# Gate and up of a ternary feed-forward with the weights stationary: the hidden layer comes out with its units on the partitions

## The chip, the cores and the metric

The kernel runs on one core of a Trainium2 chip. The metric is device time in microseconds (us) of one execution, taken as the median of several. Lower is better.

## The reference

16 sequences of 100 tokens (T = 1600 tokens, 512 features) pass a cross-attention and then a feed-forward layer; the change is in the feed-forward alone.

```python
x = x + _L0_xattn_ref(_layernorm(x), ctx_1024, ...)       # 16 heads of 128, 361 keys
x = x + _L0_ffn_ref(_layernorm(x), w_gate, w_up, w_down)  # 512 -> 2048 -> 512

def act_quant(x):      # per token, 8 bits
    scale = 127.0 / jnp.clip(jnp.max(jnp.abs(x), axis=-1, keepdims=True), EPS)
    return jnp.clip(jnp.round(x * scale), -128.0, 127.0) / scale
def weight_quant(w):   # one scale for the matrix, values -1, 0, 1
    scale = jnp.clip(jnp.mean(jnp.abs(w)), EPS)
    return jnp.clip(jnp.round(w / scale), -1.0, 1.0) * scale
def h_bitlinear(x, w): # fwht: Walsh-Hadamard transform over the whole last axis
    return jnp.einsum('bsh,oh->bso', act_quant(fwht(x)), weight_quant(w))
gate, up = h_bitlinear(h, w_gate), h_bitlinear(h, w_up)
return h_bitlinear(jax.nn.silu(gate) * up, w_down)
```

So after gate and up the hidden layer (2048 units for each token) is itself Hadamard-transformed, scaled by the largest value of each token, rounded to 8-bit integers, and multiplied by the ternary down weights.

## The kernel before, in words

Three stages follow each other: the queries, the attention, and `feed_forward` (L1254), which begins near 1027 us of the span. Only `feed_forward` is changed, apart from four semaphores that nobody waits for and that become one.

The feed-forward works on 12 tiles of 128 tokens and one last tile of 64 (t = 0 to 12). It is a software pipeline written out by hand. `step(i)` (one for each engine: L1463 POOL, L1618 PE, L1746 ACT, L1963 DVE) holds work of up to four tiles at once: gate and up, the hidden transform and the second rounding of tile i+1, down of tile i, residual, norm and first rounding of tile i+2, and the output projection of tile i+3. Every engine works its list in order; semaphores alone order the engines among each other.

TensorE's list in a step: `gate_up(i+1, 0..3)`, 30 matmuls of `out_proj(i+2)`, two `hidden_T`, `down(i)`, then `rotate_hidden(i+1, 0)`, `hidden_T(2)`, `rotate_hidden(1)`, `hidden_T(3)`, `norm_T(i+2)`, `rotate_hidden(2)` and `(3)`, `rotate_in(i+2)`, 12 matmuls of `out_proj(i+3)`, `q1_T(i+2)` and 6 more of `out_proj(i+3)`.

`gate_up(t, j)` (L1527) holds the turned integers q1T (128 features x 128 tokens, bf16) stationary and moves 512 columns of ternary weights (fp8) past them, 4 feature chunks for gate and 4 for up. So tokens lie on the partitions of PSUM, and the scale of a token is one number per partition. ACT takes silu of the gate bank with that scale (`silus`, L1743), and DVE multiplies the up bank by its scale and by that (`hidden`, L1898), into `hid`.

The Hadamard transform of the 2048 units is cut in two. Its upper part (which halves are added and subtracted) is done as butterflies on DVE and POOL: `rotate_within` (L1907), `rotate_pair1` (L1914) and `rotate_across` (L1920) on DVE, `rotate_pair0` (L1447, L1450) and its own `rotate_across` (L1456) on POOL. `hid` and `half_rot` are both in the SBUF tile `stage`, by which the profile names them. The lower part (256 wide) is done on PE by `rotate_hidden` (L1598) against a constant matrix, and for that the units must lie on partitions: `hidden_T` (L1588) transposes each 512 columns into the PSUM tiles psT, ACT rounds them to a high part (`high_hT`, L1689), and DVE takes the rest, psT minus the high part (`low_hT`, L1801). DVE then takes each token's peak (`peak`, L1859), `scales2` makes the scale, ACT and DVE round (`round2`, `ints2`), and a DMA turns the integers for `down`.

DVE's list behind the butterflies: residual and statistics of tile i+2, `low_hT(0)`, `norm`, `rotate_halves` (xr, L1832), `low_hT(1)`, `peak(0)`, `low_hT(2)`, `peak(1)`, `low_hT(3)`, `low_xT`, `peak(2)`, `peak(3)`, `scales1(i+2)`, `scales2(i+1)`, `ints1`, `ints2`. POOL's list: `rotate_pair0`, `rotate_across`, the inverse deviation (L1423), `low_o(i+3)` (L1428, the low part of the attention's output, 2048 values on each partition, released by `rotate_halves`), `result` (L1461) and two copies.

The last tile has 64 tokens: `gate_up_halves` (L1557) puts two halves of the units side by side in the array, `hidden_T_halves` (L1566) turns them.

Of the kernel before, what the change touches and what calls it, by code (L numbers as in the profile page):

```python
# [53 lines left out]
def build(nc, x, ctxT, ctx_k, wq, wk, wv, wo, gq, gk, w_ff, ident_in, had_in, out):  # L54
# [4 lines left out]
    with ExitStack() as top:  # L59
# [10 lines left out]
        passed = {e: sem(e + "_passed") for e in ("sp", "act", "dve", "pe")}  # L70
# [1183 lines left out]
def feed_forward(nc, sbt, sem, passed, bank0, ident, neg_half, w127, o_in, d_stored, d_first, x, x_in, xT0, wo_hi, wo_lo, had_in, o_dram,  # L1254
# [10 lines left out]
    with ExitStack() as ctx:  # L1265
# [13 lines left out]
        al, ald = sb("al", [P, 2]), sb("ald", [P, 1])  # L1279
# [21 lines left out]
        p_out, p_xT, p_rx, p_q1T, p_gu, p_hT, p_rh, p_down = (  # L1301
            s(f"p3_{n}") for n in ("out", "xT", "rx", "q1T", "gu", "hT", "rh", "down"))
# [5 lines left out]
        a_q1T, a_sil, v_h, g_pair0, v_pair1, v_r2, g_r2 = (s(n) for n in ("a3_q1T", "a3_sil", "v3_h", "g3_pair0", "v3_pair1",  # L1308
                                                                                  "v3_r2", "g3_r2"))
        v_cross, a_half = s("v3_cross"), s("a3_half")  # L1310
# [106 lines left out]
        def _(pool):  # L1417
# [61 lines left out]
        def _(pe):  # L1479
# [37 lines left out]
            def q1_T(t):  # L1517
# [3 lines left out]
                if due(t * NB):  # L1521
                    pe.wait_ge(v_hT, t * NB)
                for c in range(DC):
                    last = nc.tensor.transpose(psTb[1][:, c * P:(c + 1) * P], q1[:, c * P:(c + 1) * P], ident_b[:])
                last.then_inc(p_q1T, 1)

            def gate_up(t, j):  # L1527
# [18 lines left out]
            def gate_up_halves(t, j):  # L1546

                if j == 0:
                    pe.wait_ge(a_q1T, t + 1)
                pe.wait_ge(a_mag[1], 2 * t - 1 + j)  # L1550
                pe.wait_ge(v_h, t * NB + j - 1)
                apart(pe, pe_passed)
                for k in range(2):
                    for c in range(DC):
                        for g in range(2):
                            col = (j + g * NB // 2) * DIM
                            last = nc.tensor.matmul(psB[g * TH:(g + 1) * TH, 2 * j + k, :], q1T[:, c, g * TH:(g + 1) * TH],  # L1557
                                                    wt[:, k, c, col:col + DIM], start=(c == 0), stop=(c == DC - 1),
                                                    tile_position=(0, g * TH))
                last.then_inc(p_gu, 1)  # L1560

            def hidden_T_halves(t, n):
                pe.wait_ge(v_pair1, t * 6 + 5 + n)
                pe.wait_ge(a_q1T, t + 1)
                for c in range(DC):
                    last = nc.tensor.transpose(psT[n][:, c * P:(c + 1) * P], hid[:, n, c * P:(c + 1) * P], ident[:])  # L1566
                last.then_inc(p_hT, 1)
# [11 lines left out]

            def hidden_T(t, n):  # L1580
                if n % 2 == 0:
                    pe.wait_ge(g_r2 if n else v_r2, t + 1)
                if n < 2:
                    pe.wait_ge(a_q1T, t + 1)
                else:
                    pe.wait_ge(v_hT, t * NB + n - 1)
                for c in range(DC):
                    last = nc.tensor.transpose(psT[n % 2][:, c * P:(c + 1) * P], half_rot[:, n, c * P:(c + 1) * P], ident[:])  # L1588
                last.then_inc(p_hT, 1)
# [28 lines left out]
            def step(i):  # L1618
                if isinstance(i, int) and i == -2:
# [3 lines left out]
                    q1_T(0)  # L1623
                    out_proj(1, range(9, FIRST))
                    return
                if i == TILES - 2:
                    for j in range(NB // 2):
                        gate_up_halves(i + 1, j)
                    busy(psA, 7)
                    down(i, 0, TILES)  # L1630
                    hidden_T_halves(i + 1, 0)
                    hidden_T_halves(i + 1, 1)
# [36 lines left out]
                if real(i + 2):  # L1669
                    q1_T(i + 2)  # L1670
                if real(i + 3):
# [6 lines left out]
        def _(act):  # L1678
# [13 lines left out]
            def copy_half(t, n):  # L1692
                act.wait_ge(p_hT, t * NB + n + 1)
                nc.scalar.activation(hid[:, 2 + n, 0:DIM // 2].rearrange("p (c t) -> p c t", t=TH),  # L1694
                                     psT[n][:].rearrange("p (c g t) -> p c g t", g=2, t=TH)[:, :, 1, :], ACT.Copy
                                     ).then_inc(a_half, 1)

            def high_halves(t, n):
                act.wait_ge(v_cross, 2 * n + 2)
                if n == 0:  # L1700
                    act.wait_ge(p_rh, t * NB)
                nc.scalar.activation(hT_hi[:, n * DC:(n + 1) * DC, :].rearrange("p c t -> p (c t)"), half_rot[:, 2 + n, :],  # L1702
                                     ACT.Copy).then_inc(a_hT, 1)
# [7 lines left out]
            def round1(t):  # L1711
                act.wait_ge(v_scale[0], 5 * t + 4)
# [11 lines left out]

            def copy_q1T(t):
                act.wait_ge(p_q1T, t + 1)
                if due(t * NB):
                    act.wait_ge(p_gu, t * NB)
# [8 lines left out]
            def silus(t, blocks):  # L1737
                act.wait_ge(v_scale[0], 5 * t + 5)
                for j in blocks:
                    act.wait_ge(p_gu, t * NB + j + 1)  # L1740
                    if due(t * NB + j - 1):
                        act.wait_ge(v_h, t * NB + j - 1)
                    nc.scalar.activation(sil[:, j % 2, :], psB[:, 2 * (j % 2), :], ACT.Silu, scale=al[:, 0:1]  # L1743
                                         ).then_inc(a_sil, 1)

            def step(i):  # L1746
                if i == TILES - 2:
                    silus(i + 1, range(NB // 2))
                    for n in range(NB // 2):
                        copy_half(i + 1, n)  # L1750
                    for n in range(NB // 2):
                        high_halves(i + 1, n)
# [3 lines left out]
                for j in range(NB):  # L1756
                    if real(i + 1):
                        silus(i + 1, (j,))
# [5 lines left out]
                if real(i) and not last_tile(i):  # L1764
                    scale_down(i)
                if real(i + 1):
                    high_hT(i + 1, 2)
                    high_hT(i + 1, 3)
                if real(i + 2) and i > -2:
# [18 lines left out]
        def _(dve):  # L1788
# [50 lines left out]
            def scales(i, t, peaks, n, factor, weight):  # L1839

                c = slice(i, i + 1)
                norm_n = float(n) ** -0.5
                if due(t * (i + 1)):
                    dve.wait_ge(a_mag[i], t * (i + 1))
                nc.vector.tensor_reduce(mx[:, c], peaks, axis=AX.X, op=ALU.max, apply_absolute_value=True).then_inc(v_scale[i], 1)
                dve.wait_ge(v_scale[i], 5 * t + 1)
                nc.vector.tensor_scalar(am[:, c], mx[:, c], norm_n, EPS, ALU.mult, ALU.max).then_inc(v_scale[i], 1)
                dve.wait_ge(v_scale[i], 5 * t + 2)
                nc.vector.reciprocal(rc[:, c], am[:, c]).then_inc(v_scale[i], 1)
                dve.wait_ge(v_scale[i], 5 * t + 3)  # L1850
                nc.vector.tensor_scalar(sq[:, c], rc[:, c], 127.0 * norm_n, None, ALU.mult).then_inc(v_scale[i], 1)
                nc.vector.tensor_scalar(factor, weight, am[:, c], None, ALU.mult).then_inc(v_scale[i], 1)
# [204 lines left out]
```

## Time and profile before

| | |
|---|---|
| median of 3 runs | 1418.27 us (1416.5 to 1418.69) |
| span of the profiled execution | 1415.7 us |
| its granted TensorE clock | mean 0.994 |
| PE busy | 1384.3 us, 98% of the span |
| DVE busy | 933.8 us, 66% |
| ACT busy | 940.2 us, 66% |
| POOL busy | 517.2 us, 37% |
| the feed-forward | from 1027 us to the end |

The profile gives no time of its own for the profiled execution besides its span from the first to the last instruction; the median of the runs is 2.6 us above that span. A busy share says how long an engine had an instruction under way. Matmuls overlap in it: their ends are modelled, so what one costs is the distance between two starts. In a row of the timeline the first number is the start, the second the time to the end of the last instruction of the row, "x8" the number of instructions merged, and the bracket the idle time before it with the instruction that ended it. In a row of windows the numbers are the busy time of each engine with its count of instructions, then the granted TensorE clock (1.00 is full speed), the DMA share and GB/s.

### The profile page before, as it was taken

The numbers are of one execution on the slowest core, as the hardware profiler recorded it, in microseconds if no ns is written. First come the engines' busy times: TensorE is split into PE (matmuls) and PEld (weight loads), VectorE is DVE, ScalarE is ACT, GpSimd is POOL, SyncE is SP. The second block draws the span as 40 slices with busy tenths as digits, with TensorE's granted clock in tenths as the row PEclk, the third lists the DMA queues.
The fourth block names the chain that finished last, engine by engine and source line by source line (L and its number), as shares of the span: only waits on it lengthen the run. The fifth ranks groups of instructions, "written<-read, shape, count | busy, mean of one in ns | idle before, by whom it ended". The sixth has DMA issues, their size and how long they took to land. (4 is left out here: it accounts for less than half of the span.)

```text
span 1415.7 us, 25806 instructions
## 1 busy us (share of the span) xinstructions
PE 1384.3 (98%) x8407; PEld 1192.2 (84%) x8407; DVE 933.8 (66%) x2399; ACT 940.2 (66%) x2072; POOL 517.2 (37%) x323
## 2 busy tenths in 40 slices
PE   8999988999999999999999999999989999999998
PEld 8889867999999999999999999998867677776775
DVE  5222036667777777777777777766457677776775
ACT  4566558888888888888888888887533433343332
POOL 0033324432233223332323332324645465655551
PEclk9999999999999999999999999999989999999999
DMA  6867823334443443444344344325443322233211
GB/s 219 215 189 220 226 54 91 100 111 117 128 112 114 134 128 114 116 124 134 107 124 117 113 133 128 106 82 172 126 153 79 86 60 67 61 97 75 60 30 42
DMA packets 173492, 165.05 MB, mean 117 GB/s; under 512 B 81440, under 2 KB 149040, under 8 KB 171568
## 3 DMA queue, kind: packets, MB, share of 16 engines
q1 hardware_dynamic: 166448, 150.82, 38.5%
q10 hardware_dynamic: 6912, 12.59, 2.7%
q8 instruction: 69, 1.13, 0.3%
q14 instruction: 63, 0.52, 0.1%
HBM read 123.44 MB, written 33.01 MB: 111 GB/s over the span
## 5 line engine op out<-in xcount | busy, mean ns | idle before, releaser
L764 POOL TENSOR_TENSOR rk_sp<-ms_sp,neg_half 76x10 f32<-76x10 f32 (+1 forms) x128 | 238.5, 1880 | 567.0 <-DMA ms_sp<-ms 567.0
L1194 DVE CUSTOM_DVE_ANT_0 sc<-psS,rk 100x361 f32<-100x361 f32 x256 | 136.4, 533 | 97.1 <-PE psS L839 71.3
L986 ACT ACTIVATE pr<-ex,ri 100x361 f32<-100x361 f32 x256 | 153.6, 600 | 63.6 <-DVE ri L1184 63.6
L979 ACT ACTIVATE ex<-sc,nb,rq_all 100x361 f32<-100x361 f32 x256 | 175.9, 687 | 7.8 <-DVE nb L1203 7.8
L867 PE MATMUL psZ<-pT_hi,cK_hi 120*128 120x400 f32 (+1 forms) x384 | 133.3, 347 | 0.0
L867 PE MATMUL psZ<-pT_hi,cK_lo 120*128 120x400 f32 (+1 forms) x384 | 132.4, 345 | 0.0
L867 PE MATMUL psZ<-pT_lo,cK_hi 120*128 120x400 f32 (+1 forms) x384 | 132.2, 344 | 0.0
L852 PEld LDWEIGHTS psP<-ident,pr 100*120 100x120 f32 (+1 forms) x768 | 80.2, 165 | 43.5 <-issue 35.3
L839 PE MATMUL psS<-ring_hi,q_hi 128*100 128x362 f32 x256 | 97.0, 379 | 5.0 <-DVE mx L1194 5.0
L852 PE MATMUL psP<-ident,pr 100*120 100x100 f32 (+1 forms) x768 | 96.5, 261 | 4.0 <-ACT pr L986 4.0
L1176 DVE TENSOR_TENSOR pT_lo<-psP,pT_hi 121x600 fp32r<-121x600 f32 x128 | 99.0, 773 | 1.5 <-ACT pT_hi L1010 1.5
L882 PE MATMUL psNV<-z,wv_sb 128*128 128x200 f32 x504 | 97.2, 336 | 0.8 <-issue 0.8
L1184 DVE RECIPROCAL ri<-rs 100x1 f32<-100x1 f32 x256 | 41.3, 161 | 85.5 <-ACT ex L979 81.5
L1689 ACT ACTIVATE hT_hi<-psT 128x512 fp32r<-128x512 f32 x48 | 27.5, 596 | 99.8 <-PE psT L1588 99.8
L961 ACT ACTIVATE ring_hi<-bank 128x362 fp32r<-128x362 f32 x128 | 60.6, 473 | 44.1 <-PE bank L815 42.6
L1542 PE MATMUL psB<-wt,q1T 128*128 128x512 fp8e4 x384 | 86.6, 379 | 0.0
L815 PE MATMUL bank<-cT_hi,wk_hi 128*128 128x362 f32 x256 | 85.3, 333 | 1.0 <-DVE ring_lo L1129 1.0
L815 PE MATMUL psK<-cT_hi,wk_hi 128*128 128x362 f32 x256 | 85.0, 332 | 0.7 <-DVE ring_lo L1129 0.7
L1010 ACT ACTIVATE pT_hi<-psP 121x600 fp32r<-121x600 f32 x128 | 84.7, 662 | 0.0
L882 PEld LDWEIGHTS psNV<-z,wv_sb 128*128 128x128 f32 x504 | 83.0, 190 | 1.2 <-issue 1.1
L839 PE MATMUL psS<-ring_hi,q_lo 128*100 128x362 f32 x256 | 84.0, 328 | 0.0
L839 PE MATMUL psS<-ring_lo,q_hi 128*100 128x362 f32 x256 | 83.9, 328 | 0.0
(295 smaller groups left out, 3947.6 us busy)
## 6 DMA issues: line engine op xcount, KB each, us to landing
rk<-rk_dram SPq DMA_DIRECT2D x64, 564.1 KB
q_dram<-q_out SPq DMA_DIRECT2D x64, 200.0 KB, 4.3
q_in<-q_dram SPq DMA_DIRECT2D x64, 200.0 KB, 5.2
o_dram<-o SPq DMA_DIRECT2D x64, 200.0 KB, 5.4
stage<-in_w_ff SPq DMA_DIRECT2D x12, 1024.0 KB, 6.3
w_in<-in_w_ff ACTq DMA_DIRECT2D x48, 256.0 KB, 2.4
o_in<-o_dram SPq DMA_DIRECT2D x12, 1024.0 KB, 5.9
cT_in<-in_ctxT SPq DMA_DIRECT2D x15, 361.0 KB, 5.4
```

What stands on the lines that cost most here:

```text
L764: nc.gpsimd.tensor_tensor(rk_sp[:, cols], ms_sp[:, cols], neg_half[0:HG * SKR, :].to_broadcast([HG * SKR, n]), op=ALU.pow).then_inc(g_rk, 1)
L815: last = nc.tensor.matmul(psK[h % 2][:, 0:SKP], w[:, c, col:col + D], x[:, slot, c, :], start=(n == 0), stop=(n == 3 * CC - 1))
L839: last = nc.tensor.matmul(psS[0:SQ, 0:SKP], w[:, u % 2, cols], x[:, u % NG, h, :], start=(i == 0), stop=(i == 2))
L852: last = nc.tensor.transpose(psP[0:KW[i], k, i * SQ:(i + 1) * SQ], pr[:, 2 * half + k, KO[i]:KO[i] + KW[i]], ident[0:SQ, 0:SQ])
L867: last = nc.tensor.matmul(psZ[c][:, 0:UQ], w[0:KW[i], b % 2, i, c * P:(c + 1) * P], x[0:KW[i], u % 2, i, :], start=(n == 0), stop=(n == 8))
L882: last = nc.tensor.matmul(bank[:, k * 2 * SQ:(k + 1) * 2 * SQ], wv_sb[:, c, col:col + D], z[:, first % 4:first % 4 + 2, c, h * SQ:(h + 1) ...
L979: nc.scalar.activation(ex[:, h % 2, :], sc[:, h % 2, :], ACT.Exp, bias=nb[:, h % 2:h % 2 + 1], scale=factor(n), accum_out=rs[:, h % 2:h % ...
L986: nc.scalar.activation(pr[:, h, :], ex[:, h % 2, :], ACT.Copy, scale=ri[:, h % 2:h % 2 + 1]).then_inc(a_pr, 1)
L1010: nc.scalar.activation(two_heads(pT_hi, u, half), psP[0:KW[0], :, 0:3 * SQ].rearrange("p k (i q) -> p k i q", q=SQ), ACT.Copy).then_inc(a_ ...
L1176: nc.vector.tensor_tensor(two_heads(pT_lo, u, half), psP[0:KW[0], :, 0:3 * SQ].rearrange("p k (i q) -> p k i q", q=SQ), two_heads(pT_hi, u ...
L1194: nc.vector.tensor_tensor_reduce(out=sc[:, h % 2, :], in0=psS[0:SQ, 0:SK], in1=rk[:, u % 2, h, :], scale=1.0, scalar=-3.0e38, op0=ALU.mult ...
L1542: last = nc.tensor.matmul(psB[:, 2 * (j % 2) + k, :], q1T[:, c, :], wt[:, k, c, j * DIM:(j + 1) * DIM], start=(c == 0), stop=(c == DC - 1))
```

## The change

Gate and up now hold 128 x 128 of the ternary weights stationary and move the 128 columns of turned integers. A PSUM bank holds four blocks of 128 units x 128 tokens, so units lie on partitions. All `hidden_T`, `hidden_T_halves` and `copy_half` go. The token's scale now varies along the free axis: `scales1` writes it as 128 equal columns (`al_rows`), PE transposes that once for each tile (`al_T`), ACT copies it out (`alT`), DVE multiplies the gate bank by it (`gate`), ACT takes silu within SBUF, and DVE multiplies by the up bank. Up's own scale is left out of the hidden layer and put into `scales2`, by one number per token (`al_up`). The butterflies work on the same places as before. `high_hT` and `low_hT` read `half_rot` in SBUF instead of psT in PSUM. On DVE `low_hT(0)` stands ahead of the residual and `low_hT(1)` ahead of `norm`; on ACT `scale_down` stands behind `high_hT(2)` and `(3)`. The last tile uses the same `gate_up` with 64 moving columns, and does two more butterflies on DVE instead of its transposes.

```diff
+            def al_T(t):
+                pe.wait_ge(v_scale[0], 6 * t + 6)
...
+                nc.tensor.transpose(psT[0][:, 0:TT], al_rows[:], ident[:]).then_inc(p_alT, 1)
 def gate_up(t, j):
...
-                for k in range(2):
-                    for c in range(DC):
-                        last = nc.tensor.matmul(psB[:, 2 * (j % 2) + k, :], q1T[:, c, :],
-                                                wt[:, k, c, j * DIM:(j + 1) * DIM], start=(c == 0), stop=(c == DC - 1))
-                last.then_inc(p_gu, 1)
+                width, chunks = (TH, FC // 2) if last_tile(t) else (TT, FC // NB)
+                for k, done in enumerate((p_gate, p_up)):
+                    for i in range(chunks):
+                        col = (j * chunks + i) * P
+                        for c in range(DC):
+                            last = nc.tensor.matmul(psB[:, 2 * (j % 2) + k, i * width:(i + 1) * width], wt[:, k, c, col:col + P],
+                                                    q1T[:, c, 0:width], start=(c == 0), stop=(c == DC - 1))
+                    last.then_inc(done, 1)
-            def hidden_T(t, n):
...
             def high_hT(t, n):
-                act.wait_ge(p_hT, t * NB + n + 1)
+                    act.wait_ge(g_r2 if n >= 2 else v_r2, t + 1)
...
-                                     psT[n % 2][:], ACT.Copy).then_inc(a_hT, 1)
+                                     half_rot[:, 2 + n if last_tile(t) else n, :], ACT.Copy).then_inc(a_hT, 1)
             def low_hT(t, n):
                 dve.wait_ge(a_hT, t * NB + n + 1)
-                nc.vector.tensor_tensor(hT_lo[:, n * DC:(n + 1) * DC, :].rearrange("p c t -> p (c t)"), psT[n % 2][:],
-                                        hT_hi[:, n * DC:(n + 1) * DC, :].rearrange("p c t -> p (c t)").bitcast(F32),
-                                        ALU.subtract).then_inc(v_hT, 1)
+                nc.vector.tensor_tensor(lo, half_rot[:, 2 + n if last_tile(t) else n, :], hi.bitcast(F32), ALU.subtract
+                                        ).then_inc(v_hT, 1)
+            def silu(t, j):
+                act.wait_ge(v_g, t * NB + j + 1)
+                nc.scalar.activation(sil[:, j % 2, :], sil[:, j % 2, :], ACT.Silu).then_inc(a_sil, 1)
+            def gate(t, j):
+                dve.wait_ge(p_gate, t * NB + j + 1)
+                dve.wait_ge(a_alT, t + 1)
...
+                nc.vector.tensor_tensor(sil[:, j % 2, :]..., psB[:, 2 * (j % 2), :]..., alT[...].to_broadcast(...), ALU.mult)
             def hidden(t, j):
+                dve.wait_ge(p_up, t * NB + j + 1)
                 dve.wait_ge(a_sil, t * NB + j + 1)
...
+                nc.vector.tensor_tensor(hid[:, j, :], psB[:, 2 * (j % 2) + 1, :], sil[:, j % 2, :], ALU.mult).then_inc(v_h, 1)
 DVE step:
                     for n in range(3):
+                        gate(i + 1, n)
                         hidden(i + 1, n)
+                    gate(i + 1, 3)
                     rotate_within(i + 1, 2)
...
+                if real(i + 1):
+                    low_hT(i + 1, 0)
                 if real(i + 2):
                     residual(i + 2)
                 if real(i + 1):
-                    low_hT(i + 1, 0)
+                    low_hT(i + 1, 1)
                 if real(i + 2):
                     norm(i + 2)
                     rotate_halves(i + 2)
                 if real(i + 1):
-                    low_hT(i + 1, 1)
                     peak(i + 1, 0)
                     low_hT(i + 1, 2)
```

## Rows read from the trace of the kernel before

**Rows 1.** Busy time in a window of the steady feed-forward.
```profile
1220.00:1250.00 30.00, 29.98 (x165) 20.92 (x164) 21.91 (x41) 11.30 (x15) 16.55 (x11) 1.00 0.28 71
```

**Rows 2.** PE in order of time, one step from one gate_up to the next.
```profile
1215.37 7.22 PE L1542 MATMUL psB<-wt,q1T 128*128 128x512 fp8e4 x32
1222.24 0.58 PE L1491 MATMUL bank<-wk_hi,o_hi 128*128 128x512 f32 x1
...
1229.42 1.03 PE L1588 MATMUL psT<-ident,stage 128*128 128x128 f32 x8
1230.30 3.62 PE L1608 MATMUL psF<-wt,q2T 128*128 128x512 fp8e4 x16
1233.56 0.47 PE L1598 MATMUL psB<-had,hT_hi 128*128 128x256 f32 x1
...
1234.69 0.60 PE L1588 MATMUL psT<-ident,stage 128*128 128x128 f32 x4
1235.04 0.36 PE L1598 MATMUL psB<-had,hT_hi 128*128 128x256 f32 x1
...
1236.08 0.60 PE L1588 MATMUL psT<-ident,stage 128*128 128x128 f32 x4
...
1236.87 0.37 PE L1598 MATMUL psB<-had,hT_hi 128*128 128x256 f32 x1
...
1238.09 0.39 PE L1598 MATMUL psB<-had,hT_hi 128*128 128x256 f32 x1
...
1242.83 0.40 PE L1524 MATMUL psT<-ident_b,q 128*128 128x128 bf16 x4
1243.03 0.47 PE L1491 MATMUL bank<-wk_hi,o_hi 128*128 128x512 f32 x1
...
1244.51 7.22 PE L1542 MATMUL psB<-wt,q1T 128*128 128x512 fp8e4 x32
```

**Rows 3.** DVE in order of time in the same step.
```profile
1221.67 0.75 DVE L1898 SCALAR_TENSOR_TENSOR stage<-psB,al,sil 128x512 f32<-128x512 f32 x1 [1.11 <-ACT sil L1743]
1222.46 2.40 DVE L1907 TENSOR_TENSOR stage<-stage 128x256 f32<-128x256 f32 x2
...
1227.98 1.22 DVE L1920 TENSOR_TENSOR stage<-stage 128x1024 f32<-128x1024 f32 x1
1229.62 0.69 DVE L1811 TENSOR_TENSOR x<-bank,x_in 128x512 f32<-128x512 f32 x1 [0.42 <-PE bank L1491]
...
1231.48 0.68 DVE L1801 TENSOR_TENSOR hT_lo<-psT,hT_hi 128x512 fp32r<-128x512 f32 x1
...
1232.80 0.76 DVE L1832 TENSOR_TENSOR xr<-xn 128x256 f32<-128x256 f32 x2
```

**Rows 4.** POOL in order of time in the same step.
```profile
1220.64 2.50 POOL L1447 TENSOR_TENSOR stage<-stage 128x512 f32<-128x512 f32 x2 [8.91 <-DVE stage L1898]
1228.03 3.41 POOL L1456 TENSOR_TENSOR stage<-stage 128x1024 f32<-128x1024 f32 x1 [2.02 <-DVE stage L1914]
1233.71 4.59 POOL L1428 TENSOR_TENSOR o_lo<-o_in,o_hi 128x2048 fp32r<-128x2048 f32 x1 [1.52 <-DVE xr L1832]
1238.26 1.30 POOL L1461 TENSOR_TENSOR y<-y,x 128x512 f32<-128x512 f32 x1
```

**Rows 5.** Groups by line from 1010 us on: busy us, mean ns | idle before.
```profile
L1743 ACT ACTIVATE sil<-psB,al 128x512 f32<-128x512 f32 x50 | 34.4, 688 | 60.3 <-PE psB L1542 41.2 <-issue 18.1 <-PE psB L1557 1.0
```

**Rows 6.** DVE, then POOL, in the attention: a subtraction of two SBUF tiles.
```profile
984.96 1.47 DVE L1142 TENSOR_TENSOR cT_lo<-o_in,cT_hi 128x512 fp32r<-128x512 f32 x1
...
984.58 1.29 POOL L780 TENSOR_TENSOR wk_lo<-w_in,wk_hi 128x512 fp32r<-128x512 f32 x1
```

**Rows 7.** PE in order of time: the last tile's gate and up.
```profile
1389.83 3.64 PE L1557 MATMUL psB<-wt,q1T 128*64 128x512 fp8e4 x32 [0.87 <-ACT q1T L1729]
```

**Rows 8.** Windows: PE idle in the first step, and the clock after it.
```profile
1052.00:1054.00 2.00, 0.00 (x0) 0.00 (x0) 1.97 (x3) 0.00 (x0) 1.03 (x1) 1.00 0.00 0
1056.00:1058.00 2.00, 1.35 (x6) 1.35 (x7) 1.63 (x4) 2.00 (x2) 0.89 (x2) 0.50 0.34 118
```

More of the change, by code:

```diff
@@ L69, in build @@
         d_wo = [sem(f"d_wo{i}") for i in range(5)]
-        passed = {e: sem(e + "_passed") for e in ("sp", "act", "dve", "pe")}
+        passed = dict.fromkeys(("sp", "act", "dve", "pe"), sem("passed"))
         ident = sbt(top, "ident", [P, P])
@@ L1278, in feed_forward @@
         mx, am, rc, sq = (sb(n, [P, 2]) for n in ("mx3", "am3", "rc3", "sq3"))
-        al, ald = sb("al", [P, 2]), sb("ald", [P, 1])
+        al_rows, alT, al_up, ald = sb("al_rows", [P, TT]), sb("alT", [P, TT]), sb("al_up", [P, 2]), sb("ald", [P, 1])
         mag1, mag2 = sb("mag1", [P, DIM]), sb("mag2", [P, FF])
@@ L1300, in feed_forward @@
         a_o, v_o, g_o = s("a3_o"), s("v3_o"), s("g3_o")
-        p_out, p_xT, p_rx, p_q1T, p_gu, p_hT, p_rh, p_down = (
-            s(f"p3_{n}") for n in ("out", "xT", "rx", "q1T", "gu", "hT", "rh", "down"))
+        p_out, p_xT, p_rx, p_q1T, p_alT, p_gate, p_up, p_rh, p_down = (
+            s(f"p3_{n}") for n in ("out", "xT", "rx", "q1T", "alT", "gate", "up", "rh", "down"))
         v_x1, v_st, g_rs, v_xn, v_xr = (s(n) for n in ("v3_x1", "v3_st", "g3_rs", "v3_xn", "v3_xr"))
@@ L1578, in down_halves @@
                 last.then_inc(p_down, 1)
-            def hidden_T(t, n):
[L1581 to L1589, printed above, removed]
             def rotate_hidden(t, n):
@@ L1623, in step @@
                     q1_T(0)
+                    al_T(0)
                     out_proj(1, range(9, FIRST))
@@ L1670, in step @@
                     q1_T(i + 2)
+                    al_T(i + 2)
                 if real(i + 3):
@@ L1723, in round2, with copy_alT @@
                                      bias=MAGIC, scale=sq[:, 1:2]).then_inc(a_mag[1], 1)
+            def copy_alT(t):
+                act.wait_ge(p_alT, t + 1)
+                if due(t * NB):
+                    act.wait_ge(v_g, t * NB)
+                nc.scalar.activation(alT[:], psT[0][:, 0:TT], ACT.Copy).then_inc(a_alT, 1)
             def copy_q1T(t):
@@ L1735, in scale_down @@
                 nc.scalar.activation(y[:], psF[:], ACT.Copy, scale=ald[:]).then_inc(a_y, 1)
[L1737 to L1744, printed above, removed]
+            def silu(t, j):
+                act.wait_ge(v_g, t * NB + j + 1)
+                nc.scalar.activation(sil[:, j % 2, :], sil[:, j % 2, :], ACT.Silu).then_inc(a_sil, 1)
             def step(i):
                 if i == TILES - 2:
-                    silus(i + 1, range(NB // 2))
+                    for j in range(NB // 2):
+                        silu(i + 1, j)
                     for n in range(NB // 2):
-                        copy_half(i + 1, n)
-                    for n in range(NB // 2):
-                        high_halves(i + 1, n)
+                        high_hT(i + 1, n)
                     scale_down(i)
@@ L1757, in step @@
                     if real(i + 1):
-                        silus(i + 1, (j,))
+                        silu(i + 1, j)
                 if real(i + 1):
@@ L1763, in step @@
                     high_o(i + 3)
-                if real(i) and not last_tile(i):
-                    scale_down(i)
                 if real(i + 1):
@@ L1768, in step @@
                     high_hT(i + 1, 3)
+                if real(i) and not last_tile(i):
+                    scale_down(i)
                 if real(i + 2) and i > -2:
@@ L1966, in step @@
                 if i == TILES - 2:
+                    gate(i + 1, 0)
                     hidden(i + 1, 0)
+                    gate(i + 1, 1)
                     rotate_within(i + 1, 0)
@@ L1999, in step @@
                     return
+                if real(i + 1):
+                    low_hT(i + 1, 0)
                 if real(i + 2):
@@ L2002, in step @@
                 if real(i + 1):
-                    low_hT(i + 1, 0)
+                    low_hT(i + 1, 1)
                 if real(i + 2):
```

156 lines of the change are left out of this document (64 added, 92 removed).

## The prediction

> **What bounds the kernel now.** I read the busy time by windows first: in the feed-forward PE is busy 29.98 of 30.00 us, with DVE at 21.9 and POOL at 16.6 [rows 1]. A full window may be a modelled one, so next I laid PE's list out in time [rows 2]. One step is 29.14 us (1215.37 to 1244.51) and has no idle entry: PE bounds it. I call its start G and give times from it. gate_up takes 6.87 (to 1222.24), out_proj 7.18, two hidden_T 0.88, down 3.26; then rotate_hidden and the other transposes alternate. Last I read DVE and POOL for how much room stands before PE's waits [rows 3, 4]. There is little: DVE's last butterfly ends at 1229.20, G+13.8, and PE uses it at G+14.05. DVE's xr ends at G+18.2, and 0.15 us later POOL begins o_lo, which takes 4.59 us.
>
> **The change, PE's work.** Removed are the transposes [rows 2]: 8 in 0.88 us, and 4 in 1235.04 - 1234.69 = 0.35, and 4 more that I take at the same: 1.6 us a step. Added is al_T, one transpose, 0.1. gate_up turns from 32 matmuls of 512 columns into 128 of 128 columns, each with its own weight load. The trace has such a pair only as the transposes of q1: four in 1243.03 - 1242.83 = 0.20 us, 0.05 each; spread over the pipeline I take 0.056, so 7.2 us against 6.87, +0.3. Bounds: 0.05 is 6.4 us. If the load hid nothing, twice 0.056, it is 14.3, +7.5. If PE alone counted, a step would be 29.14 - 1.6 + 0.1 + 0.3 = 27.9.
>
> The Trainium skill (TensorE: Matmul & The Clock Gate, "Back-to-back issue gap") speaks against that: a sustained stream of load and matmul pairs at 128 columns is put at about 81 ns a matmul. By it gate_up would be 10.4 us, 3.2 more than by the row of q1; no row here holds more than four such pairs in a run.
>
> **DVE, ACT and POOL before the transform.** Each of the four blocks now has a chain gate (0.70), silu (0.69) [rows 5], multiplication (0.70, against 0.75) [rows 3], with gate j+1 slipped in behind multiplication j: about 2.08 us a block on DVE, where PE needs 1.8. The first gate starts at 16 x 0.056 + 0.27 = G+1.2. The multiplications end at G+3.4, 5.5 and 7.5. PE's fourth block waits for the second of them, 0.15 us. The third ended at G+7.05 before (1221.67 + 0.75) [rows 3]. From there to the end of the last butterfly were 6.8 us, partly waits for POOL, which the fourth gate fits into: the last butterfly ends at G+14.4. POOL's rotate_across then runs to G+16.6 (G+16.07 before) [rows 4].
>
> **The part that decides: low_hT reads two SBUF tiles.** Before, its inputs were psT in PSUM and hT_hi in SBUF. What a DVE instruction with two SBUF inputs suffers beside POOL is seen three times. First, DVE's 256-element butterflies, two in 2.40 us where xr's same shape takes 0.76 for two, while POOL runs L1447 and its successors [rows 3, 4]. Second, POOL's L1456 takes 3.41 for 1024 elements, where o_lo takes 4.59 for 2048; it began 0.05 us after DVE's 1.22 us L1920, so 1.1 us of it is waiting [rows 3, 4]. Third, a DVE subtraction of exactly low_hT's kind started at 984.96, POOL's had run from 984.58 to 985.87, and DVE's took 1.47 us, which is 0.91 until POOL's end and 0.56 after it [rows 6]. With one input in PSUM there is none of this: L1811 took 0.69 beside L1456, and low_hT itself 0.68 [rows 3, 4]. So whoever starts first keeps the other out until its end.
>
> The Trainium skill (SBUF — State Buffer, "Who interferes with whom") says the same of two SBUF inputs, and adds what the rows, with at most 1.3 us of POOL in one piece, leave open: the pair is held for the whole instruction, so it would be held for all of a 4.59 us one. The sum below does not need the page; the bound without it is the second rival.
>
> Carried through DVE's new list:
> - low_hT(0): high_hT(0), one pass of ACT over 128 x 512 (0.69 at most) [rows 5], ends at 15.1, POOL holds until 16.6, so it ends at 17.3. PE arrives at 7.3 + 7.2 + 3.3 = 17.8. Hidden.
> - the residual now starts behind it, at 17.1 (before at G+14.25). 1.86 us later (1231.48 - 1229.62) [rows 3] comes low_hT(1), which ends at 19.6; PE wanted it at 17.8 + 1.1 = 18.9: 0.8 of stall.
> - from the residual's start to xr's end were 3.94 us (1229.62 to 1233.56) with one low_hT between, as now: xr ends at G+21.0, 2.8 later than before. POOL starts o_lo 0.1 later, at 21.1.
> - peak(0) keeps DVE until 21.5. low_hT(2) comes 0.4 us after o_lo has begun and waits until 25.7, ending at 26.3. rotate_hidden(2) starts at 26.35 instead of 1236.87, G+21.5 [rows 2].
> - POOL's next, result (1.30) [rows 4], has been waiting and takes its turn at 26.2, until 27.5. low_hT(3), behind peak(1), ends at 28.2. rotate_hidden(3) starts at 28.25 instead of 1238.09, G+22.7.
> - from there to the next G were 6.4 us (1244.51 - 1238.09); al_rows, one more DVE instruction before q1, and al_T make it 6.9.
>
> The step becomes 28.25 + 6.9 = 35.1, 6.0 longer. PE's saved 1.2 us lies inside its wait and is worth nothing.
>
> **The clock.** PE now stands idle some 5 us in each step (21.4 to 26.35). In the first step of before, PE did nothing from 1052 to 1054 at the full clock, and at 1056 to 1058 the granted clock was 0.50, the lower level of 1.2 GHz [rows 8]. So I expect the lower level for part of what follows. If 3.5 us run at it, rotate_hidden(3), rotate_in and out_proj lose some 1.1 us of path; if 7 us, 2.5; if the level holds, nothing. I take 1.1: the step is 36.2, 7.1 longer.
>
> **The sum.** o_lo is in 11 steps (tiles 2 to 12): 11 x 7.1 = 78. The step after them, without o_lo, still has the late residual and POOL's result: +2. The last tile's gate and up were 32 half-width matmuls in 3.64 us [rows 7]; now 128 of 64 columns with full loads, which I put at 0.056 too, 7.2. Its second gate, silu and multiplication end 3 us later, and what follows (more butterflies, fewer transposes) costs the same: +2.9; with 0.03 a pair nothing, with 0.1 about 8. al_T(0) and the like at the start: +0.2. Together +83: span 1415.7 + 83 = 1499. The median of the runs stood 2.6 above the span: 1501. The four semaphores made one cost nothing, nobody waits for them. The moved scale_down waits for PE anyway, and POOL's result behind it is held by o_lo. DMAs are the same in number and their queue has slack of several us before each use.
>
> **The rivals.**
> 1. Faster: low_hT is not held up, for a reason the rows don't show. Then DVE's list ends in time, and the step lies between 27.9 (PE's sum) and 28.7 (with low_hT(1) and the two late norm steps on the path). It decides if low_hT(2) is done by G+20.5. 12 steps x 1.2 = 15 less, at least 12 x 0.45 = 5; with +2.9 for the last tile: 1406 to 1416. For it: low_hT took 0.68 beside POOL in every step before; but that was with PSUM. Against it: the subtraction of [rows 6].
> 2. Only part of the hold-up: DVE gets ahead of o_lo, or is not held for all of it. Low_hT(2) needs to start 0.4 us earlier or o_lo later. Then the step is about 31.5: 11 x 2.4 + 5 = +31, 1449. Against it: o_lo followed xr by 0.15 us, and peak(0) stands between on DVE.
> 3. The weight load does not hide. At 0.1 a pair gate_up takes 12.8; the wait for low_hT doesn't cover it, since DVE's chain starts later too. Of its 5.6 us over the forecast's 7.2 about half reach the path, since DVE needs 2.08 a block anyway: the step becomes 39, 10 longer, 11 x 10 + 10 = +120, 1538. With no hold-up at low_hT it would be +57. Against it: four transposes in 0.20 [rows 2].
>
> The 81 ns of the Trainium skill (TensorE: Matmul & The Clock Gate, "Back-to-back issue gap") are this third rival in a milder form: by them the step would be 1.7 longer than forecast, 1522 in all, and their chance is in its 0.10.
>
> **How the numbers follow.** Forecast 0.70, rival 1 0.12 (0.07 of it beyond 0.2%, which is about what a measurement of this kernel can tell from no change, 0.05 within), rival 2 0.08, rival 3 0.10. The forecast's own range is from no fall of the clock (11 x 6.0 + 5 = +71, 1489) to 7 us of it (11 x 8.5 + 5 = +99, 1517), with an error of 1 us a step in my chain on the low side: 1475 to 1520. To hold eight in ten it must reach towards rivals 2 and 3: 1468 to 1532. Faster 0.07, same 0.05, slower 0.88. The predicted time is the forecast's, 1501.
>
> **What would show it.** Right: low_hT in SBUF form with two of four instances of well over 1 us a step, one of about 4.8; rotate_hidden(3) some 28 us behind gate_up; PE's share in the steady windows down from 100% to about 85%, with granted clock below 1.00; 128 gate and up matmuls in 7.2 us; o_lo still 4.59. Wrong: low_hT at 0.7 everywhere; steps below 29 us (rival 1); gate_up over 10 us (rival 3); o_lo longer and low_hT short, which means that DVE went first (rival 2).

## The result: 5.9% slower, and the profile after

The changed kernel takes 1500.58 us (median of 4 runs, 1499.57 to 1502.07) against 1417.38 of the kernel before in the same series: a ratio of 1.0587, 95% interval 1.0566 to 1.0608. The forecast was 1501 us. The span of the profiled execution is 1497.8 us, 82.1 more than before, and its mean granted clock is 0.970.

First the step that is shown below, from one gate_up to the next, then a window of 30 us, in the columns of [rows 1].

```profile
1184.99:1220.47 35.48, 29.62 (x243) 24.31 (x242) 28.85 (x45) 11.17 (x17) 17.48 (x10) 0.95 0.24 60
1190.00:1220.00 30.00, 24.14 (x153) 19.11 (x151) 25.87 (x41) 8.89 (x14) 17.48 (x10) 0.94 0.19 53
```

PE was busy 29.98 of 30 us [rows 1] and is now busy 29.62 of the 35.48 us of a step, 83%. The window of 30 us shows less, 24, since it holds PE's whole wait but not a whole step of its work. DVE was busy 21.36 us in a step and is now busy 28.85. What PE waits for most stands in these rows of the waits after the change (engine, what waits <- for what: total us, times, longest).

```profile
PEld psB L1573 <- DVE hT_lo L1763: 70.0, 26, 5.7
PE psB L1573 <- DVE hT_lo L1763: 63.4, 25, 5.3
PE bank L1498 <- DVE xr L1793: 8.0, 11, 2.2
```

PE and its weight loads wait above all for one thing, low_hT (L1763). The first two rows are the same stretches, once for the loads and once for the matmuls, so they do not add up. The same step as in [rows 2], here from 1184.99 to 1220.47; first PE, then DVE, then POOL in order of time.

```profile
1202.51 0.47 PE L1573 MATMUL psB<-had,hT_hi 128*128 128x256 f32 x1
...
1204.41 0.39 PE L1573 MATMUL psB<-had,hT_hi 128*128 128x256 f32 x1 [0.60 <-DVE hT_lo L1763]
...
1206.20 0.66 PE L1498 MATMUL bank<-ident,xr 128*128 128x128 f32 x4 [0.58 <-DVE xr L1793]
1211.38 0.58 PE L1573 MATMUL psB<-had,hT_hi 128*128 128x256 f32 x1 [4.53 <-DVE hT_lo L1763]
...
1213.26 0.41 PE L1573 MATMUL psB<-had,hT_hi 128*128 128x256 f32 x1
...
1220.47 7.45 PE L1551 MATMUL psB<-q1T,wt 128*128 128x128 bf16 x128
```
```profile
1199.84 2.08 DVE L1763 TENSOR_TENSOR hT_lo<-stage,hT_hi 128x512 fp32r<-128x512 f32 x1 [0.70 <-ACT hT_hi L1662]
...
1203.68 0.68 DVE L1763 TENSOR_TENSOR hT_lo<-stage,hT_hi 128x512 fp32r<-128x512 f32 x1
...
1205.38 0.76 DVE L1793 TENSOR_TENSOR xr<-xn 128x256 f32<-128x256 f32 x2
1206.06 0.69 DVE L1840 TENSOR_REDUCE mx<-psB 128x1 f32<-128x512 f32 x1
1206.66 4.67 DVE L1763 TENSOR_TENSOR hT_lo<-stage,hT_hi 128x512 fp32r<-128x512 f32 x1
1211.25 0.68 DVE L1840 TENSOR_REDUCE mx<-psB 128x1 f32<-128x512 f32 x1
1211.86 1.15 DVE L1763 TENSOR_TENSOR hT_lo<-stage,hT_hi 128x512 fp32r<-128x512 f32 x1
```
```profile
1197.96 3.40 POOL L1455 TENSOR_TENSOR stage<-stage 128x1024 f32<-128x1024 f32 x1 [2.02 <-DVE stage L1892]
...
1206.29 4.50 POOL L1427 TENSOR_TENSOR o_lo<-o_in,o_hi 128x2048 fp32r<-128x2048 f32 x1 [1.52 <-DVE xr L1793]
1210.74 1.72 POOL L1460 TENSOR_TENSOR y<-y,x 128x512 f32<-128x512 f32 x1
```

Read the ends. low_hT(0) ends at 1201.92, 0.56 us after POOL's L1455 (1201.36). low_hT(2) began 0.37 us after o_lo and ends at 1211.33, 0.54 after it (1210.79). Then low_hT(2), which had been waiting, went first, POOL's addition to y waited (1.72 instead of the 1.30 of [rows 4]), and low_hT(3) ends at 1213.01, 0.55 after that addition (1212.46). So each ends some 0.55 us behind the POOL instruction that it met; the rest of 2.08, 4.67 and 1.15 is waiting. low_hT(1), which started before any POOL instruction, took 0.68. Over all 50 instances the mean is 1.99 us, where it was 0.68 [rows 3].

The 82.1 us by place, from the starts of gate_up. The first was at 1040.31 and is at 1039.69: -0.6. Eleven steps were 29.16 us each and are 36.18: 77.2. The twelfth, which has no o_lo, was 28.72 and is 33.62: +4.9. From the last tile's gate_up to the end: 25.87 and now 26.48: +0.6.

### The profile page after: what moved, and what is told of

Read it like the earlier page. It is cut to its first block and busy times, and to the rows that moved or that the text cites. A ratio compares the mean times of both kernels' runs of the same rounds, so it can differ in the third digit from the quotient of the medians.

```text
span 1497.8 us, 28048 instructions
## 1 busy us (share of the span) xinstructions
PE 1396.1 (93%) x9468; PEld 1243.8 (83%) x9468; DVE 1023.2 (68%) x2462; ACT 937.2 (63%) x2083; POOL 529.1 (35%) x323
## 5 line engine op out<-in xcount | busy, mean ns | idle before, releaser
L1573 PE MATMUL psB<-had,hT_hi 128*128 128x256 f32 x200 | 72.2, 377 | 63.5 <-DVE hT_lo L1763 63.4
L1573 PEld LDWEIGHTS psB<-had,hT_hi 128*128 128x128 f32 x200 | 51.5, 257 | 71.3 <-DVE hT_lo L1763 70.0
L1763 DVE TENSOR_TENSOR hT_lo<-stage,hT_hi 128x512 fp32r<-128x512 f32 x50 | 99.4, 1989 | 9.1 <-ACT hT_hi L1662 9.1
L1551 PEld LDWEIGHTS psB<-q1T,wt 128*128 128x128 fp8e4 x1664 | 89.8, 98 | 5.6 <-issue 4.2
L1551 PE MATMUL psB<-q1T,wt 128*128 128x128 bf16 (+1 forms) x1664 | 93.2, 217 | 0.8 <-ACT q1T L1695 0.8
L1675 ACT ACTIVATE mag<-psF,sq 128x512 f32<-128x512 f32 x13 | 8.9, 688 | 123.4 <-DVE sq L1812 123.4
```

The costliest lines, as they stand in the source:

```text
L1551: last = nc.tensor.matmul(psB[:, 2 * (j % 2) + k, i * width:(i + 1) * width], wt[:, k, c, col:col + P], q1T[:, c, 0:width], start=(c == 0) ...
L1573: last = nc.tensor.matmul(psB[:, n, k * HB:(k + 1) * HB], m[:, n * DC + k * HC + c, :], had[:, c, :], start=(c == 0 and m is hT_hi), stop= ...
L1763: nc.vector.tensor_tensor(lo, half_rot[:, 2 + n if last_tile(t) else n, :], hi.bitcast(F32), ALU.subtract).then_inc(v_hT, 1)
```

## The experiments

The mean step below is that over the first eleven steps of each kernel's profiled execution; it was 29.16 before and 36.18 after. Two kinds of explanation are told apart. My theory: a DVE instruction with two SBUF inputs is kept out while a POOL instruction runs, and o_lo is the long one. The rivals: the new chain of gate, silu and multiplication, the turned matmuls, or DVE's new order.

**One: two SBUF inputs alone, in the kernel before.**

```diff
-                nc.vector.tensor_tensor(hT_lo[:, n * DC:(n + 1) * DC, :].rearrange("p c t -> p (c t)"), psT[n % 2][:],
+                nc.vector.tensor_tensor(hT_lo[:, n * DC:(n + 1) * DC, :].rearrange("p c t -> p (c t)"), wo_hi[0][:, n, :].bitcast(F32),
```

> The kernel before, with one edit: low_hT takes its minuend from a fixed SBUF tile (the output weights) instead of psT in PSUM, so the low part of the hidden layer is not the right one. Transposes, gate and up and every order stay. Theory (a DVE instruction with two SBUF inputs waits until POOL's running one ends): low_hT(1) now comes just ahead of o_lo, low_hT(2) waits some 2.7 us behind it, low_hT(3) behind POOL's next; the step grows from 29.1 to between 32.6 and 33.7 us, 11 steps, so +38 to +50 us, 1455 to 1467. Rival (the loss comes from the chain gate, silu, multiplication or from DVE's new order): no change, 1417.

Measured: 1460.54 us, ratio 1.0337 (1.0313 to 1.0361); mean step 33.45. This changes no matmul and no order, only where one operand lies. (The tile is wo_hi in the kernel; the profile calls it wk_hi.) DVE's and POOL's rows of one step, which starts at 1207.21:

```profile
1223.31 0.68 DVE L1801 TENSOR_TENSOR hT_lo<-wk_hi,hT_hi 128x512 fp32r<-128x512 f32 x1
1225.02 0.76 DVE L1832 TENSOR_TENSOR xr<-xn 128x256 f32<-128x256 f32 x2
1225.70 0.68 DVE L1801 TENSOR_TENSOR hT_lo<-wk_hi,hT_hi 128x512 fp32r<-128x512 f32 x1
1227.81 3.53 DVE L1801 TENSOR_TENSOR hT_lo<-wk_hi,hT_hi 128x512 fp32r<-128x512 f32 x1 [0.38 <-ACT hT_hi L1689]
1231.86 1.16 DVE L1801 TENSOR_TENSOR hT_lo<-wk_hi,hT_hi 128x512 fp32r<-128x512 f32 x1
...
1225.92 4.87 POOL L1428 TENSOR_TENSOR o_lo<-o_in,o_hi 128x2048 fp32r<-128x2048 f32 x1 [1.52 <-DVE xr L1832]
1230.74 1.74 POOL L1461 TENSOR_TENSOR y<-y,x 128x512 f32<-128x512 f32 x1
```

The second low_hT came 0.22 us ahead of o_lo and was not delayed; o_lo took 4.87 instead of 4.59, so this time POOL waited. The third came into o_lo and ended 0.55 after it.

The one operand gives 4.3 of the 7.0 us by which a step grew. The other 2.7 belong to the changed order of DVE together with that operand: here low_hT(0) began at 1223.31, when POOL's L1456 was just over, and xr ended 18.6 us behind gate_up. In the changed kernel low_hT(0) met POOL's L1455, the residual stood behind it, and xr ended after 21.15 us, 2.6 later.

**Two: one PSUM input, in the changed kernel.**

```diff
-                nc.vector.tensor_tensor(lo, half_rot[:, 2 + n if last_tile(t) else n, :], hi.bitcast(F32), ALU.subtract
+                still = psT[1][:, 256:512].unsqueeze(1).to_broadcast([P, 2, 256])
+                lo, hi = (a.rearrange("p (k j) -> p k j", j=256) for a in (lo, hi))
+                nc.vector.tensor_tensor(lo, still, hi.bitcast(F32), ALU.subtract).then_inc(v_hT, 1)
```

> The changed kernel, with one edit: low_hT takes its minuend from a bank of PSUM that nothing writes (256 columns read twice) instead of half_rot in SBUF, so the low part is not the right one. All waits stay. Theory (two SBUF inputs): every low_hT is 0.7 us again, the step falls from 36.2 to between 28.7 and 29.6 us, PE is nearly full and the granted clock stays at 1.00; in all 1408 to 1422. Rival (DVE's chain of gate, silu and multiplication is what makes the step long): the step stays above 33, over 1465.

Measured: 1412.36 us, ratio 0.9984 (0.9972 to 0.9996); mean step 28.85. The group of low_hT in this kernel (columns as in [rows 5]):

```profile
L1765 DVE TENSOR_TENSOR hT_lo<-psT,hT_hi 128x512 fp32r<-128x512 f32 x50 | 34.1, 685 | 9.1 <-ACT hT_hi L1662 9.1
```

So the whole loss hangs on this one operand; the rest of the change comes out even, or 0.16% better. The chain of gate and silu, DVE's order and the turned matmuls are all still in this kernel. Together they take back 0.9 of the 1.2 us a step that PE's sum saves, and no more.

**Three: matmuls in PE's idle time, in the changed kernel.**

```diff
                 if real(i + 1):
+                    busy(psT[1], 21)
                     rotate_hidden(i + 1, 2)
```

> The changed kernel, with 21 matmuls of 512 columns into an idle bank between norm_T and rotate_hidden(2), 4.5 us, where PE waits for low_hT(2). Theory (PE's idle time lets the clock fall, and that costs 1.1 us of each step): granted clock near 1.00 in the steady windows, low_hT unchanged at 4.7 us, the step 35.1 instead of 36.2, so -12 us, 1488. Rival (PE is not on the path at the lower clock, DVE alone sets the step): same time within 3 us.

Measured: 1489.11 us, ratio 1.053 (1.0513 to 1.0546), against 1.0587 without the filler: 0.0057 of 1415 is 8 us, where 12 were expected. The mean step is 34.98, 1.20 less, 13 us over eleven; the twelfth step, where there is little idle time to fill, is 38.12 instead of 33.62 and gives 4.5 back. Three windows of the changed kernel around a wait, and one of a whole step with the filler:

```profile
1205.00:1211.00 6.00, 1.27 (x10) 0.83 (x8) 5.96 (x5) 0.60 (x1) 4.71 (x2) 0.99 0.00 1
1211.00:1214.00 3.00, 2.62 (x12) 2.62 (x13) 3.00 (x5) 0.00 (x0) 2.88 (x3) 0.50 0.56 156
1214.00:1218.00 4.00, 4.00 (x25) 3.58 (x25) 2.85 (x12) 0.69 (x1) 0.15 (x1) 0.96 0.78 211
```
```profile
1205.00:1240.00 35.00, 33.32 (x262) 26.91 (x262) 28.95 (x47) 11.16 (x16) 17.61 (x11) 1.00 0.26 61
```

After the wait rotate_hidden runs at a granted clock of 0.50, the lower level of 1.2 GHz, and with the filler the clock stays at 1.00. That is the clock's term: 1.2 us a step in the mean.

The steps differ in it. With the filler the eleven steps, but for the first, are 35.0 to 35.2 us. Two steps without it, and the one shown in the result as a third:

```profile
1112.58:1148.32 35.74, 30.00 (x242) 24.68 (x242) 28.85 (x45) 11.06 (x17) 17.49 (x10) 0.90 0.28 60
1148.32:1184.99 36.67, 30.66 (x243) 25.35 (x242) 28.83 (x45) 11.14 (x17) 17.48 (x10) 0.91 0.27 59
```

The third took 35.48 us at a mean clock of 0.95. Since the granted clock was either 1.00 or 0.50, these means say that the lower level lasted some 7, 7 and 3.5 us. Against the steps with the filler it cost 0.7, 1.7 and 0.5 us. The first two differ in where it fell: in the first it began 3 us ahead of rotate_hidden(2) (1138.90), while PE was still waiting. Of the eleven steps two are like the first and two like the third; six are like the second, with 36.4 to 36.7 us; the very first has 36.3, with a clock of 0.81.

**Four: the turned matmuls alone, in the kernel before.**

```diff
-                    for c in range(DC):
-                        last = nc.tensor.matmul(psB[:, 2 * (j % 2) + k, :], q1T[:, c, :],
-                                                wt[:, k, c, j * DIM:(j + 1) * DIM], start=(c == 0), stop=(c == DC - 1))
+                    for i in range(FC // NB):
+                        col = (j * (FC // NB) + i) * P
+                        for c in range(DC):
+                            last = nc.tensor.matmul(psB[:, 2 * (j % 2) + k, i * TT:(i + 1) * TT], wt[:, k, c, col:col + P],
+                                                    q1T[:, c, :], start=(c == 0), stop=(c == DC - 1))
```

> The kernel before, with gate_up alone turned: 128 matmuls of 128 columns with 128 loads of ternary weights for each full tile, everything else left, so the layout of the hidden layer does not fit what follows. Theory (the load hides beside the matmul before it, 0.057 a pair): gate_up 7.3 us instead of 6.87, the step 29.5 instead of 29.1, so +5 us, 1422. Rival (loads don't hide in a long run or run out of instructions, 0.08 or more a pair): +3.4 us a step or more, over 1455.

Measured: 1416.3 us, ratio 1.0018 (1.0007 to 1.0029); mean step 29.28, +0.12. The row of its gate and up:

```profile
1211.80 7.40 PE L1544 MATMUL psB<-q1T,wt 128*128 128x128 bf16 x128
```

The last of 128 starts 7.40 - 0.22 us behind the first, so a pair costs 7.18 / 127 = 0.0565 us. The whole is 0.3 us longer than the 32 matmuls of before [rows 2], though it has 128 loads instead of 32, so the loads hide throughout. The step grew by less than that, 0.12 where 0.4 was expected; where the other 0.2 us went was not followed.

**Five: low_hT ahead of xr, in the changed kernel.** The same instructions in another order.

```diff
-                if real(i + 1):
-                    low_hT(i + 1, 0)
                 if real(i + 2):
                     residual(i + 2)
                 if real(i + 1):
-                    low_hT(i + 1, 1)
+                    for n in range(NB):
+                        low_hT(i + 1, n)
                 if real(i + 2):
                     norm(i + 2)
                     rotate_halves(i + 2)
                 if real(i + 1):
                     peak(i + 1, 0)
-                    low_hT(i + 1, 2)
                     peak(i + 1, 1)
-                    low_hT(i + 1, 3)
```

> The changed kernel with one change in DVE's list: residual, then low_hT(0) to (3), then norm and rotate_halves, then the peaks. So all four low_hT are done before xr releases o_lo; number and form of the instructions stay. Theory (the place of low_hT against o_lo decides): low_hT about 0.7 us, but for the first behind POOL's rotate_across; the step 29.5 to 30 us, in all 1420 to 1430. Rival (two SBUF inputs are slow beside any POOL work, wherever they stand): more than 33 us a step, over 1465.

Measured: 1422.3 us, ratio 1.0058 (1.0044 to 1.0073); mean step 29.58.

```profile
1232.68 2.58 DVE L1763 TENSOR_TENSOR hT_lo<-stage,hT_hi 128x512 fp32r<-128x512 f32 x4
1235.74 0.76 DVE L1793 TENSOR_TENSOR xr<-xn 128x256 f32<-128x256 f32 x2
...
1229.24 3.41 POOL L1455 TENSOR_TENSOR stage<-stage 128x1024 f32<-128x1024 f32 x1 [2.02 <-DVE stage L1892]
1236.65 4.57 POOL L1427 TENSOR_TENSOR o_lo<-o_in,o_hi 128x2048 fp32r<-128x2048 f32 x1 [2.88 <-DVE xr L1793]
```

Four low_hT in 2.58 us, with two SBUF inputs each, since they lie in the gap between POOL's L1455 (over at 1232.65) and o_lo. The form of the operand is no price by itself; only the meeting is. The step is 0.4 us above the one before, and PE now has another wait in all eleven steps: the output projection needs o_lo, which xr releases, and xr ends 20.2 us behind gate_up instead of 18.2.

```profile
1241.27 0.50 PE L1490 MATMUL bank<-wk_hi,o_hi 128*128 128x512 f32 x1 [1.20 <-POOL o_lo L1427]
```

**Six: a quarter of o_lo, in the changed kernel.**

```diff
-                nc.gpsimd.tensor_tensor(o_lo[:], o_in[:], o_hi[:].bitcast(F32), op=ALU.subtract).then_inc(g_o, 1)
+                nc.gpsimd.tensor_tensor(o_lo[:, 0:OH, :], o_in[:, 0:OH, :], o_hi[:, 0:OH, :].bitcast(F32), op=ALU.subtract
+                                        ).then_inc(g_o, 1)
```

> The changed kernel with POOL's o_lo over a quarter of its elements (512 of 2048 on each partition); the other three quarters of the attention's low part are left out. Theory (POOL holds DVE out for the whole of its instruction): low_hT(2) takes 0.7 to 1.3 us instead of 4.7, about 3.4 us shorter, as o_lo itself is; the step 31.5 to 32.5 instead of 36.2, in all 1445 to 1460. Rival (a fixed price of each meeting, whatever the length): low_hT(2) stays near 4.7 and the time near 1500.

Measured: 1456.21 us, ratio 1.0291 (1.0272 to 1.031); mean step 32.42. low_hT(2) and o_lo in one step:

```profile
1223.16 1.44 DVE L1764 TENSOR_TENSOR hT_lo<-stage,hT_hi 128x512 fp32r<-128x512 f32 x1
1225.12 1.17 DVE L1764 TENSOR_TENSOR hT_lo<-stage,hT_hi 128x512 fp32r<-128x512 f32 x1
...
1222.79 1.27 POOL L1427 TENSOR_TENSOR o_lo<-o_in,o_hi 128x512 fp32r<-128x512 f32 x1 [1.52 <-DVE xr L1794]
1224.01 1.73 POOL L1461 TENSOR_TENSOR y<-y,x 128x512 f32<-128x512 f32 x1
```

o_lo is 3.2 us shorter (4.50 to 1.27), low_hT(2) 3.2 us (4.67 to 1.44). The hold-up is as long as what is left of POOL's instruction. The step gains 3.8, the 0.6 beyond that by my reckoning at the clock, whose mean was 0.95 to 1.00 in all steps but the first. Of the 3.3 us that are left, 0.7 are still the clock: the four steps at 1.00 are 31.7 us in the mean. The others go with low_hT(0) behind L1455, the residual behind it, what is left of low_hT(2)'s wait, and low_hT(3) behind POOL's addition, as in the rows of the result; no run parts them.

**Seven and eight: repairs.** Seven is the order of five, with high_o behind high_hT(3) on ACT, and o_lo in four pieces, each released by itself:

```diff
+                for k in range(NO):
+                    heads = slice(k * OH, (k + 1) * OH)
+                    nc.gpsimd.tensor_tensor(o_lo[:, heads, :], o_in[:, heads, :], o_hi[:, heads, :].bitcast(F32),
+                                            op=ALU.subtract).then_inc(g_o, 1)
...
+                    if not first and h % OH == 0:
+                        pe.wait_ge(g_o, (t - 2) * NO + h // OH + 1)
```

> A repair: the order of the kernel with all four low_hT before norm, high_o behind high_hT(3) on ACT, and o_lo in four pieces of 512 with a release each, so that the output projection waits for its own quarter alone. Theory: low_hT near 0.7 us, the step 28.6 to 29, in all 1407 to 1418, like the run with the PSUM operand. Rival (late xr costs as much as low_hT gains): step over 29.5, 1425 or more.

Measured: 1410.09 us, ratio 0.9976 (0.9966 to 0.9986); mean step 28.60. The one long DVE row and o_lo's pieces:

```profile
1224.33 2.48 DVE L1767 TENSOR_TENSOR hT_lo<-stage,hT_hi 128x512 fp32r<-128x512 f32 x4
...
1228.21 5.04 POOL L1429 TENSOR_TENSOR o_lo<-o_in,o_hi 128x512 fp32r<-128x512 f32 x4 [2.79 <-DVE xr L1797]
```

Eight adds another order of PE's and DVE's work on the four blocks:

```diff
-                for j in range(NB):
+                for j, part in ((0, 0), (1, 0), (0, 1), (1, 1), (2, 0), (3, 0), (2, 1), (3, 1)):
                     if real(i + 1):
-                        gate_up(i + 1, j)
+                        gate_up(i + 1, j, part)
...
+                elif due(t * NB + j - 1):
+                    pe.wait_ge(v_g, t * NB + j - 1)
```

> The same repair, and PE does gate blocks 0 and 1, then up 0 and 1, then gate 2 and 3, up 2 and 3; DVE takes gates and multiplications in that order, and PE's second pair waits for the gates alone to free its banks. Theory (DVE's bubbles for silu, 0.75 us a block, go, and the butterflies end earlier): the step 28.2 to 28.8, in all 1402 to 1412, faster than before. Rival (those bubbles were covered by the waits for POOL): same as the run without it, within 2 us.

Measured: 1408.74 us, ratio 0.9959 (0.9946 to 0.9972); mean step 28.53. The number lies in the theory's range too, but the intervals of seven and eight overlap, so they are not told apart, and that is the rival's outcome. The butterflies did start earlier, 7.2 us behind gate_up instead of 7.9, and ended no earlier (14.1 in both), since the first pair took longer while POOL ran its own butterflies. Seven, then eight:

```profile
1215.98 1.85 DVE L1889 TENSOR_TENSOR stage<-stage 128x256 f32<-128x256 f32 x2
```
```profile
1215.92 2.96 DVE L1894 TENSOR_TENSOR stage<-stage 128x256 f32<-128x256 f32 x2
```

In both kernels PE's waits in a step are the ones for the integers q1 and for xr, as in these rows of seven:

```profile
1206.37 0.40 PE L1527 MATMUL psT<-ident_b,q 128*128 128x128 bf16 x4 [0.47 <-DVE q L1848]
...
1228.12 0.66 PE L1502 MATMUL bank<-ident,xr 128*128 128x128 f32 x4 [0.31 <-DVE xr L1797]
```

Both beat the kernel before, by 0.24% and 0.41%. That is little: the kernel before itself came out at 1417.38, 1414.73 and 1414.22 us in the three series, and only the ratios within a series compare. Turned matmuls and repairs together are worth that much, not the 1.2 us a step of PE's own sum. What the repairs alone would bring to the kernel before was not run.

Seven changes three things at once. The order is worth most, as five shows. From five to seven the step falls by another 1.0 us, and PE's wait of 1.20 us for o_lo is gone; whether the four pieces or the later high_o did that was not parted.

## Why the prediction was right

- **That PE's saving is worth nothing.** PE's sum fell as worked out: gate_up 7.2 us (0.0565 a pair, in experiment four), the transposes gone. The step is set elsewhere, and even with low_hT free of waits (two) it is 28.85 and not 27.9.
- **The chain before the transform.** The last butterfly was put at G+14.4; in the step after 1220.47 it ends at G+14.1. POOL's L1455 was put at G+16.6 and ends at G+16.4 (1236.82 in the trace of after, a step later than the rows shown).
- **low_hT held out.** In the step shown, G = 1184.99: xr ends at G+21.15 (forecast 21.0), low_hT(2) at 26.34 (26.3), rotate_hidden(2) starts at 26.39 (26.35), rotate_hidden(3) at 28.27 (28.25). Experiments one and two, from both sides, show the cause; five shows that it is the meeting and six that the length of POOL's instruction is the price. The Trainium skill (SBUF — State Buffer, "Who interferes with whom") states the one thing that the rows of before left open, that whichever of the two engines comes first keeps the ports that they share for its whole instruction. The trace agrees: beside an o_lo of 4.50 us low_hT(2) took 4.67, and ended 0.54 after it. One reading of before was loose: the low_hT of [rows 3], with 0.68, began when L1456 was just over. The trace has the better row, inside o_lo (1233.71 to 1238.30):

```profile
1235.96 0.69 DVE L1801 TENSOR_TENSOR hT_lo<-psT,hT_hi 128x512 fp32r<-128x512 f32 x1 [0.38 <-ACT hT_hi L1689]
```

- **The clock: right in size, in part by luck.** Taken at 1.1 us a step, measured by three at 1.20. But the working was 3.5 us at the lower level for 1.1, or 7 for 2.5, and no row fixed how long it would last. In the trace 3.5 us cost 0.5, and most steps had some 7 us of it for 1.4 to 1.7. The duration was put too short and the cost of each us too high, and the two cancelled.
- **The step.** 36.2 forecast, 36.18 measured: 77 of 78 us over eleven steps. Without the clock it was put at 35.1, and three shows 34.98. That both agree to 0.1 us is closer than a chain of ten rounded terms can promise. The busy share of PE was put at 85% and is 83%. Two low_hT of well over 1 us were forecast for a step; 2.08 and 4.67 are these, and the fourth, with 1.15, is a little over.
- **Two small terms were off and cancelled in part.** The twelfth step was put at +2 and cost +4.9. There POOL's addition to y came early, since no o_lo stood before it, and met norm (xn), and POOL's two copies behind it met xr. PE waited 2.23 us for xr, and from 1460 to 1465 the granted clock was 0.51:

```profile
1457.51 1.49 DVE L1785 TENSOR_SCALAR xn<-x,mv,rstd 128x512 f32<-128x512 f32 x1 [0.44 <-POOL rstd L1422]
1459.04 1.46 DVE L1793 TENSOR_TENSOR xr<-xn 128x256 f32<-128x256 f32 x2
...
1457.44 1.27 POOL L1460 TENSOR_TENSOR y<-y,x 128x512 f32<-128x512 f32 x1
1458.78 0.69 POOL L1435 COPY x<-x 128x512 f32<-128x512 f32 x1
1459.53 0.69 POOL L1437 COPY x<-x 128x512 f32<-128x512 f32 x1
```

  The last tile was put at +2.9 and cost +0.6. The mis-sized term is the pair with 64 moving columns, taken at 0.056; the prediction also said that 0.03 would cost nothing:

```profile
1471.32 3.89 PE L1551 MATMUL psB<-q1T,wt 128*128 128x64 bf16 x128 [0.76 <-ACT q1T L1695]
```

  3.89 less the last one's 0.19, over 127, is 0.029 us a pair: half the columns, half the time, with the full load of 128 columns each.
- **The third rival** (loads that don't hide) is out by experiment four. The 81 ns a pair of the Trainium skill (TensorE: Matmul & The Clock Gate, "Back-to-back issue gap") did not come up: 56.5 ns a pair over 128 pairs in a run, and the measurement decides.
- **The second rival** needed low_hT(2) 0.4 us earlier. The margin was real, 0.37 us in the step shown, and experiment one has the other outcome in it, where a low_hT came 0.22 ahead of o_lo and went first.

## What to carry to other kernels

When an operand moves from PSUM to SBUF, look at what the other of DVE and POOL does at that moment: a DVE instruction with two SBUF inputs that comes second waits for the end of the POOL instruction that is running, so its price is the rest of that instruction and not its own 0.7 us. (Every POOL instruction that was met here reads SBUF; one that only writes was not tried.) Two remedies were shown alone, each against a loss of 5.9%: with such instructions placed in POOL's gaps 0.6% was left (five), and with one operand in PSUM nothing (two). A shorter POOL instruction holds DVE for less (six). Cutting it into pieces with a release each was run only together with the new order, and there it stood after all of low_hT, so that it helps DVE is not shown. And work taken off the busiest engine counts only up to the next chain: 1.2 us of PE's step saved gave 0.6 with everything repaired.

## What the runs showed of the hardware that was not expected

- A tensor_scalar of DVE with one SBUF tile as input was held out too: xn took 1.49 us beside POOL's addition in the twelfth step, against 0.55 in the other eleven, where POOL was idle. It did the same in experiments three and six.
- POOL is held as well, and even for a tiny instruction: the reciprocal deviation of one column (L1422) took 0.93 us behind low_hT(1), where it had 0.55 before. With low_hT's operand in PSUM (two) it is 0.55 again, at the same place in the list.

```profile
1203.84 0.93 POOL L1422 TENSOR_TENSOR rstd<-ve,neg_half 128x1 f32<-128x1 f32 x1 [2.48 <-DVE ve L1779]
```

- When POOL's instruction ends, a DVE instruction that has been waiting goes ahead of POOL's next: after o_lo came low_hT(2), and POOL's addition took 1.72 us instead of 1.30, in the step shown above.
- A full 128 x 128 fp8 load hides beside a matmul of only 64 columns (0.029 us a pair).
